# The perceiver attention written out as thirteen slots, with one LayerNorm for two and the query roots inside the exponential

## What is computed

```
x = x + tanh(g_xattn[2]) * L2_xattn(ctx_768, layernorm(x), mask, ...)

xn = layernorm(ctx, ln_x_g, ln_x_b)            # 96 wide
ln = layernorm(layernorm(x), ln_l_g, ln_l_b)   # 128 wide: the outer LayerNorm sees a normalised x
q  = ln @ Wq.T
kv = concat([xn @ Wkv.T, ln @ Wlkv.T], axis=1) # 256 keys per batch
qn = rmsnorm(q, qn_g) * 64**-0.5 ; kn = rmsnorm(k, kn_g)   # per head, 2 heads of 64
attn = softmax(where(mask, qn @ kn.T, -max))
out  = (attn @ v) @ Wo.T + bo
```

## Time and profile before

| | |
|---|---|
| time, median of 3 runs (lowest, highest) | 2415.44 us (2412.63, 2420.06) |
| profiled execution: its time, its span | 2403.2 us, 2401.4 us |
| mean granted TensorE clock of the span | 0.89 |
| the perceiver layer in the trace | 1361.7 to 1646.2 us, about 284.5 us, 12% of the span |
| busy in those 284.5 us: PE, DVE, ACT, POOL | 202.3, 151.7, 116.2, 77.5 us |

### The profile page before, as it was taken

The page is one execution under the profiler, slowest core; times in us unless marked ns, Lnnn a source line. Parts: engine busy times, 40 slices in busy tenths (PEclk is TensorE's granted clock), DMA queues, the critical chain, the costliest instruction groups (busy, mean ns, idle before and its releaser), DMA issues. The chain is left out here.

```text
span 2401.4 us, 49877 instructions
## 1 busy us (share of the span) xinstructions
PE 2068.9 (86%) x18068; PEld 1574.7 (66%) x18068; DVE 1609.6 (67%) x3302; ACT 1250.7 (52%) x2880; POOL 804.6 (34%) x714
## 2 busy tenths in 40 slices
PE   6669999999986989699999767776798899999964
PEld 3359999989884666466666456665575466666654
DVE  5789999999987888444444445654465566666644
ACT  3278888888834767333332134442243466656631
POOL 1124544444542333144444422221000233323233
PEclk7589999999997999899999867775599899999975
DMA  2100000000002000344435100001000000000001
GB/s 56 41 1 8 13 14 8 14 14 8 13 2 77 9 9 2 72 88 107 106 71 117 37 7 7 4 0 50 1 0 7 4 4 4 5 5 4 1 2 35
DMA packets 41412, 61.72 MB, mean 26 GB/s; under 512 B 9464, under 2 KB 18208, under 8 KB 40800
## 3 DMA queue, kind: packets, MB, share of 16 engines
q1 hardware_dynamic: 41184, 58.66, 10.1%
HBM read 56.02 MB, written 2.62 MB: 24 GB/s over the span
## 5 line engine op out<-in xcount | busy, mean ns | idle before, releaser
L827 POOL TENSOR_TENSOR a_probs<-a_probs,a_rsums 128x1024 f32<-128x1024 f32 x64 | 121.3, 1896 | 321.4 <-DVE a_rsums L875 321.4
L1504 POOL TENSOR_TENSOR f_h<-f_gated,f_w_spread 128x512 f32<-128x512 f32 x128 | 161.5, 1268 | 196.7 <-DVE f_gated L1558 93.9
L1558 DVE TENSOR_TENSOR f_gated<-f_silu,f_up 128x512 f32<-128x512 f32 x128 | 87.1, 685 | 184.4 <-PE f_up L1635 169.5
L2300 ACT ACTIVATE f_combine<-f_logits,f_neg_row_max 128x128 f32<-128x128 f32 x512 | 198.5, 395 | 0.5 <-DVE f_neg_row_max L2158 0.5
L1598 ACT ACTIVATE f_silu<-f_gate 128x512 f32<-128x512 f32 x128 | 76.2, 597 | 221.2 <-PE f_gate L1635 218.8
L2119 POOL TENSOR_TENSOR f_slot_sum<-f_slot_sum,f_logits 128x512 f32<-128x512 f32 x96 | 122.6, 1277 | 182.1 <-DVE f_slot_max L2237 99.0
L1650 PEld LDWEIGHTS f_acc<-f_down,f_h 128*128 128x128 f32 x1024 | 129.0, 192 | 42.4 <-issue 37.5
L2127 POOL TENSOR_TENSOR f_acc<-f_acc,f_row_factor 128x512 f32<-128x512 f32 x128 | 136.4, 1067 | 60.6 <-DVE f_slot_max L2237 38.5
L2361 PE MATMUL f_give_bank<-f_y,f_combineT 128*128 128x128 f32 x1024 | 140.0, 280 | 12.8 <-DVE f_y L2207 7.5
L863 DVE TENSOR_REDUCE a_negmax<-a_score_bank 128x8 f32<-128x1024 f32 x64 | 78.1, 1221 | 103.0 <-PE a_score_bank L1004 103.0
L2350 PE MATMUL f_slot_bank<-f_logits,f_xn 128*128 128x128 f32 x1024 | 137.4, 277 | 6.1 <-issue 5.1
(11 more groups left out here) (328 smaller groups left out, 5181.7 us busy)
## 6 DMA issues: line engine op xcount, KB each, us to landing
f_w_spread<-f_routing_rows SPq DMA_DIRECT2D x64, 512.0 KB, 9.9
f_w<-in_f_w SPq DMA_DIRECT2D x16, 256.0 KB, 2.5
a_cT<-in_ctxT SPq DMA_DIRECT2D x16, 192.0 KB, 2.4
f_gate_up<-in_f_guT SPq DMA_DIRECT2D x1, 2048.0 KB, 8.2
out<-x_resident SPq DMA_DIRECT2D x8, 256.0 KB, 2.4
c_cT<-in_ctxT SPq DMA_DIRECT2D x8, 192.0 KB, 2.5
a_ctx<-in_ctx SPq DMA_DIRECT2D x8, 192.0 KB, 2.6
f_phi<-in_f_phi SPq DMA_DIRECT2D x1, 1024.0 KB, 5.0
```

The costliest lines, as they stand in the source:

```text
L827: nc.gpsimd.tensor_tensor(probs[:, u], probs[:, u], rsums[:, u, :].unsqueeze(2).to_broadcast([S, 8, S]), ALU.mult).then_inc(normalised, 1)
L1504: nc.gpsimd.tensor_tensor(h[:, u % KEPT, :], gated[:, u % 2, :], w_spread[:, u // PER, u % PER, :], ALU.mult).then_inc(weighted, 1)
L2300: last = nc.scalar.activation(back[:, m % BACKS, j, :], raw[:, m % RING, j, :], ACT.Exp, bias=neg_row[:, k, b:b + 1], accum_out=row_part[: ...
```

## The change

The layer is written as thirteen slots, t from -4 to 8, with no loop. In slot t each engine does a fixed list of pieces, and each piece belongs to a group t-1, t, t+1, t+2, t+3 or t+4. Probabilities and outputs of group t-1, scores and exponentials of group t, queries and keys of group t+1, projections of group t+2, normalisation of group t+3 and statistics of group t+4 thus stand in one slot. The other edits:

- The two LayerNorms of the latents are one: the inverse root is that of `var*(1+eps) + eps*eps`, so the `a2x` statistics, roots and normalisation are gone.
- Queries are turned as they are; their inverse root is the `scale` of the exponential, and the shift is the maximum times the root. Only keys are scaled on VectorE (1024 elements in place of 1536). GpSimd takes the roots in two instructions, keys (16 columns) first.
- All four probability tiles are copied by ScalarE. The projections are copied in two pieces for each batch (128 and 512 elements) in place of four. Squares are two instructions.
- The mask is added in two instructions of 1024 elements in place of four of 512, the maxima are two in place of one.
- The scores alternate between the two heads, batch by batch.
- PSUM: scores and turned probabilities share four banks, projections have two, one `work` bank is used by five kinds of transposes in turn, one bank is for the weighed values and the output.
- The exponentials stand at the end of ScalarE's slot, the squares of group t+2 behind them.

```
-    MASKED = 3.4e38
+    MASKED = 1e30
+    SLOTS = range(-4, GROUPS + 1)
@@ latents
-                    n_x.vector_stats(dve, i, s, it)
+                    n_l.vector_stats(dve, i, s, j)
+                    nc.vector.tensor_scalar(n_l.veps[:, s, :], n_l.mv[:, s, :, 1], 1.0 + LN_EPS, LN_EPS * LN_EPS,
+                                            ALU.mult, ALU.add).then_inc(n_l.veps_done, 1)
@@ exponentials
-                            last = nc.scalar.activation(probs[:, s, h, b, :], sc[:, s, h, b, :], ACT.Exp,
-                                                        bias=negmax[:, h, b:b + 1], accum_out=psum_[:, s, b, h:h + 1])
+                            last = nc.scalar.activation(sc[:, s, h, b, :], sc[:, s, h, b, :], ACT.Exp,
+                                                        bias=shift[:, s, b, h:h + 1], scale=rn[:, s, b * H + h:b * H + h + 1],
+                                                        accum_out=totals[:, s, b, h:h + 1])
@@ projections kept
-                        nc.scalar.activation(qk[:, s, b, 0:2, :].rearrange("p c d -> p (c d)"), lat_bank(b)[:, 0:2 * D],
-                                             ACT.Copy)
-                        nc.scalar.activation(v[:, s, b, 1, :], lat_bank(b)[:, 2 * D:3 * D], ACT.Copy).then_inc(lat_kept, 1)
-                        nc.scalar.activation(qk[:, s, b, 2, :], ctx_bank(b)[:, 0:D], ACT.Copy)
-                        nc.scalar.activation(v[:, s, b, 0, :], ctx_bank(b)[:, D:2 * D], ACT.Copy).then_inc(ctx_kept, 1)
+                    nc.scalar.activation(q[:, j % 2, b, :], both[:, LAT, 0:D], ACT.Copy)
+                    nc.scalar.activation(kv[:, j % 4, b].rearrange("p c k d -> p c (k d)"), both[:, :, D:3 * D],
+                                         ACT.Copy).then_inc(kept, 1)
@@ VectorE, its whole slot
+                    if there(t - 1):
+                        invert_sums(t - 1)
+                    if there(t + 1):
+                        mean_squares(t + 1)
+                    if there(t + 3):
+                        n_l.vector_normalise(dve, *at(t + 3))
+                        n_c.vector_normalise(dve, *at(t + 3))
+                    if there(t + 4):
+                        latent_statistics(t + 4)
+                    if there(t + 1):
+                        scale_keys(t + 1)
+                    if there(t):
...
+                        mask_scores(t)
+                    if there(t - 1):
+                        normalise_outputs(t - 1)
+                    if there(t + 4):
+                        context_statistics(t + 4)
+                    if there(t - 1):
+                        update(t - 1)
@@ scores on TensorE
+                    for p in range(2):
+                        for b in (2 * p, 2 * p + 1):
+                            for h in range(H):
+                                r = slice(DH * h, DH * h + DH)
...
```

More of the change, by code:

```diff
@@ L1692, in layer4_perceiver @@
[L1692 to L1698, removed]
@@ L1730, in _ @@
[L1730 to L1742 removed]
+                nc.gpsimd.memset(neg[:, :, LAT, :], 0.0).then_inc(neg_done, 1)
@@ L1877, in _ @@
[L1877 to L1889 removed]
+                act.wait_ge(gain_done, 1)
@@ new lines, in project @@
+                def project(j, b):
+                    bs = slice(b * S, (b + 1) * S)
+                    if b == 0:
+                        pe.wait_ge(work_emptied, use["l", j] + 1)
+                    if j or b:
+                        pe.wait_ge(kept, G * j + b)
+                    nc.tensor.matmul(both[:, LAT, 0:3 * D], lT[:, j % 2, bs], wl[:, :], start=True, stop=True)
+                    nc.tensor.matmul(both[:, CTX, D:3 * D], cT[:, j % 2, bs], wc[:, :], start=True, stop=True)\
+                        .then_inc(projected, 1)
@@ new lines, in scores @@
+                def scores(j):
+                    s = j % 2
+                    pe.wait_ge(work_emptied, use["k_ctx", j] + 1)
+                    if j:
+                        pe.wait_ge(pT_done, G * j)
+                    for p in range(2):
+                        for b in (2 * p, 2 * p + 1):
+                            for h in range(H):
+                                r = slice(DH * h, DH * h + DH)
+                                first = 512 * (2 * p + h) + 256 * (b % 2)
+                                last = nc.tensor.matmul(score_bank[:, first:first + 256], qT[r, s, b, :],
+                                                        kT[r, s, b].rearrange("p c k -> p (c k)"), start=True, stop=True)
+                        last.then_inc(scored, 1)
@@ new lines, in weigh @@
+                def weigh(j, b):
+                    pe.wait_ge(pT_done, G * j + b + 1)
+                    if j and b == 0:
+                        pe.wait_ge(updated, j)
+                    for h in range(H):
+                        for c in range(2):
+                            last = nc.tensor.matmul(out_bank[:, (b * H + h) * DH:(b * H + h + 1) * DH], pT[:, b, 2 * h + c, :],
+                                                    kv[:, j % 4, b, c, 1, h * DH:(h + 1) * DH], start=c == 0, stop=c == 1)
+                    if b == G - 1:
+                        last.then_inc(weighed, 1)
```

468 lines of the change are left out of this document (224 added, 244 removed).

## The result

The changed kernel takes 2332.65 us (median of 4 runs, 2329.57 to 2336.32), the kernel before beside it 2414.03 us (2400.23 to 2420.06): ratio 0.9681, 95% interval 0.9643 to 0.9718. The forecast was 2372 us, its range 2346 to 2404. The profiled executions stand at 2403.2 and 2330.9 us, 72 us apart, and the perceiver layer accounts for 68 of these; 3 us lie in front of it and 1 us behind it, where the instructions are the same. The other 9 us up to the difference of the medians have no trace: the profiled execution of the kernel before is one of its short ones.

The account below looks back on a forecast made before the run. No engine full; a chain bounds each turn, its slow half at half clock. Filling 60, middle 164 (139.5 slots, 17.6 falls, 7 handoffs), ending 17: layer 241 against 284.5, 43 us off 2415.4, 2372 us; range 2346 to 2404.

Parts of the forecast that it names:

- The chain of a slot at full clock: Middle of the perceiver layer: from one group's first exponential through VectorE's list to the next group's, 21.4 us.
- So a fall costs 4.4 us a slot: Middle slots: TensorE's clock halves at the probabilities and returns after the scores and a projection, lengthening the slot 4.4 us.
- I take two slots in three: Middle: the share of slots taken to hold a fall, four falls of 4.4 us, 17.6 us.
- Handoffs: Middle: waits between engines that were rounded away, about 1 us in each slot, 7 us.
- Ending: Last stretch of the layer: the same chain as before at half clock, 17 us.
- Filling: Start of the layer to its first exponential: 60 us, 57.2 before.
- A: Rival for the middle: the clock never falls since bursts are mixed, 17.6 us saved, 2354 us; chance 0.17.
- B: Rival: GpSimd's roots hold VectorE's normalisations, up to 4.5 us in six slots, 27 us, 2399 us; chance 0.08.
- C: Rival: the clock stays at half through the slots, layer 285 us, no change, 2415 us; chance 0.08.
- D: Rival: half clock throughout and heads not overlapping, scores 6.9 us, TensorE the bound, 2437 us; chance 0.06.
- The signs: Expected in the profile: first exponentials alternating about 22 and 26 us, layer clock under 0.85, scores near 1.9 us, VectorE unbroken.
- about 14: VectorE's busy time a group in the middle, said to fall from 17.1 to about 14 us.

Follow-up runs that it names:

- `a_hole`: The changed kernel, but TensorE waits for all eight exponentials of a group before it turns the first probabilities: 2344.15 us.

## Why the prediction was wrong, step by step

- **The chain of a slot at full clock: right, 21.4 us with statistics and 20.8 without.** 21.2 and 20.9 us measured, through the same instructions. Inside it two prices erred against each other: an exponential costs 0.595 and not 0.49, 0.8 us a slot, and what stands from the keys to the next exponentials took 9.6 us for 10.3. The two last slots were too short (20.5 and 15.1 us for 19.5 and 14.2). At full clock the seven come to about 141 us for the 139.5 booked; of the measured 142.9 about 2 are falls.
- **"So a fall costs 4.4 us a slot": the step that failed.** "I take two slots in three" was not the error: five of the first six slots hold a fall. Its length was. I let the clock stay at half from the probabilities to the scores and a projection behind them, some 17 us, as in the old turn. Here it is at half for 3.4 us in three slots and for 6.8 and 10.2 in two. And VectorE's list hides part of what is left: forced in each slot the price is 1.1 us, while in the changed kernel the 6.8 us of the first slot cost nothing and the 10.2 us of the sixth 0.7. Booked 17.6 us, measured about 2. A fall that sits on the scores and goes on behind them does cost more, 5 to 9 us with heads apart, and the changed kernel has none. Why its falls end sooner is open: the runs show that a longer wait brings longer ones (`a_hole`) and that the heads' order matters, not what decides the length.
- **Handoffs, 7 us: too much.** About 1.5 are left when the falls are taken off. The rest I had already counted, since the durations of rows include drains that the next instruction does not wait for: the 0.7 us from the keys on show it. The two terms make 21 of the 25 us by which the layer came out shorter than forecast.
- **Ending, 17 us: 13.9.** The last weighing and output work, "the same chain, half clock", has a clock of 0.77.
- **Filling, 60 us: right** (59.4), and so were the keys' root (2.93 us for 2.9), the queries' (1.63 for 1.6), the scores (2.00 for 1.9), mask and maxima (2.35 and 2.34).
- **The rivals.** A, the clock never falls: nearest in time (2354), and too slow even so, by handoffs, ending and what lies outside the layer. B is dead: normalisations beside the roots take 1.11 and 1.05 us; it also counted six slots with normalisations in the middle, where four have them. C and D need whole slots at half clock, and the heads overlap. D priced the scores without overlap at 6.9 us at half clock; with heads apart they take 5.0 to 5.7.
- **The signs.** Two came out as written: the scores at 2.00 us and a clock of the layer under 0.85 (0.84). VectorE stops once in its list, 1.07 us for the keys' root, and the distances do not alternate between 22 and 26 us.
- **A slip without weight.** The subtractions named for VectorE take 17.1 us a group to 12.7 and not to "about 14"; the time of the chain was walked without them.
- **What I did not see in the old profile:** its half clock alone cost 37 us (layer's middle) to 45 us (medians), as much as my whole forecast saving. The earlier trace rows held that: TensorE busy 14.4 of 17.1 us at 0.50.
- **The scale.** The layer gained 68.3 us by the profiles; medians give 76 to 81. Of the extra 8 to 13 us the profiles show 4 in the layers around it, whose instructions are the same; the rest is not in the two profiled executions, and the kernel before scatters from 2400 to 2420 us.

## What to carry to other kernels

Price a fall of TensorE's clock by its length and by what is on the chain while it lasts: 17.1 us at half clock cost 5.2 us a turn where transposes and weighing were the chain; 6.8 us cost 0 to 1.9 where VectorE's list hid all or part of it, 10.2 us in a slot without projections 0.7, and 10 to 17 us that began at the scores 5 to 9. Take the length from rows of the new kernel, not of the old one. Before rebuilding a kernel whose trace shows a long dense stretch at 0.50 behind a short wait, fill that wait with spare transposes: here one edit of a few lines gave more than half of what the whole pipeline gave. In a slot scheme move what is ready ahead of what waits, then look for the next equal chain; only what both share shortens the slot.

## What the runs showed of the hardware that I had not expected

- Scores of the two heads, 64 rows each, take 2.00 us for 16 passes when alternated and 2.96 us apart, at full clock. The Trainium skill (TensorEngine Tiling (Array Packing), Key Properties) says that different tiles load and multiply in parallel; the trace agrees.
- The order of those heads also moved the clock's falls: stretches of 10 to 17 us at half clock in slots 1 to 4 with heads apart, none over 6.8 us there with heads mixed. Spare transposes before the probabilities did not cure it.
- An exponential of 128x256 with its scale from a tensor takes 595 ns, without it 504.
- Filling 3 us of idle a turn with spare transposes lifted the mean clock of the old middle from 0.74 to 0.97; in the new slots, with 1.25 us of idle there, the same filling lifted it from 0.89 to 0.93 and gained nothing.
